# A separate drain for the last batch: pairs of token tiles, other PSUM banks, stores tile by tile

## The reference, cut to what matters

```
x = x + layernorm(attention(layernorm(x)))          # x: 8 batches x 512 tokens x 256 features, float32
x = x + layernorm(ffn(layernorm(x)))

def attention(x):
    q, k, v = split(x @ W_qkv.T)                    # 16 heads of 16 features; k is normalized over its 16
    for t in range(512):                            # a scan over the tokens, F is 16 x 16 per head
        F = retention * F + coef * outer(v[t], k[t])
        y[t] = (W_LTM + F) @ q[t]
    return y @ W_o.T

def ffn(x):
    h = relu(x @ W_fc.T) ** 2                       # 1024 hidden features
    y = h @ W_proj.T
    mem = 0                                         # 5 steps of a spiking unit on each element
    for step in range(5):
        mem = 0.9 * mem + y - (mem > 1)
        spikes += (mem > 1)
    return spikes / 5
```

## Time and profile before

| | us |
|---|---|
| median of 3 runs | 639.84 (638.00 to 641.08) |
| the profiled execution | 640.17 |
| its span, first to last instruction | 638.4 |
| TensorE busy | 498.8 (78%) |
| VectorE busy | 534.7 (84%) |
| ScalarE busy | 326.7 (51%) |
| GpSimd busy | 384.3 (60%) |

### The profile page before, as it was taken

How to read it: one execution, slowest core, us unless ns; L and a number is a source line. 1 busy time by engine, 2 the same in 40 slices (tenths; PEclk the granted TensorE clock), 3 DMA queues, 4 the chain that set the end, 5 groups by cost and what they waited for, 6 DMA issues and landing times.

```text
span 638.4 us, 7784 instructions
## 1 busy us (share of the span) xinstructions
PE 498.8 (78%) x2272; PEld 326.5 (51%) x2272; DVE 534.7 (84%) x937; ACT 326.7 (51%) x637; POOL 384.3 (60%) x184
## 2 busy tenths in 40 slices
PE   3583478449996999699979997899969995895891
PEld 1341135126673657355745665566636663473670
DVE  4799989997998999899999999999899999821001
ACT  4522123245546754656376646655567355646634
POOL 0026965785567776677677767875687667811101
PEclk9875589679897999989998999798979998988796
DMA  7364476465644575456545664567338634200000
GB/s 236 114 182 134 131 212 183 119 164 146 182 128 122 165 208 139 131 140 189 167 135 156 180 180 119 154 173 209 99 85 230 203 110 132 66 2 0 32 2 33
DMA packets 54729, 87.63 MB, mean 137 GB/s; under 512 B 5408, under 2 KB 19360, under 8 KB 54688
## 3 DMA queue, kind: packets, MB, share of 16 engines
q1 hardware_dynamic: 54112, 87.12, 48.2%
q10 hardware_dynamic: 576, 0.03, 0.1%
HBM read 78.74 MB, written 8.39 MB: 136 GB/s over the span
## 4 chain that ended last, share of the span: by engine, by line
PE 53%; issue 16%; POOL 10%; ACT 10%; DVE 10%; DMA 1%; POOLq 0%; ACTq 0%; DVEq 0%
PE p_c L346 13%; PE p_c L371 12%; PE p_a L281 7%; POOL prod L875 6%; PE p_y L324 6%; DVE state L733 5%; PE p_c L337 4%; ACT sign L547 3%; PE p_c L354 2%; PE p_a L301 2%; POOL x1t L891 2%; PE p_y L319 2%; DVE p_u L723 2%; ACT oo L468 1%; PE p_c L363 1%
## 5 line engine op out<-in xcount | busy, mean ns | idle before, releaser
L875 POOL TENSOR_TENSOR prod<-state,qf 128x1024 f32<-128x1024 f32 x128 | 302.8, 2371 | 147.5 <-DVE state L733 126.1
L733 DVE TENSOR_TENSOR_SCAN state<-ret,p_u 128x512 f32<-128x512 f32 x256 | 308.8, 1207 | 0.0
L723 DVE TENSOR_TENSOR p_u<-vrep,p_k 128x512 f32<-128x512 f32 x256 | 171.1, 674 | 2.5 <-ACT p_k L479 2.5
L346 PE MATMUL p_c<-wproj_sb,ht 128*128 128x256 f32 x512 | 116.1, 382 | 1.3 <-ACT ht L537 1.3
L371 PE MATMUL p_c<-x1t,wfc_s 128*128 128x512 f32 x384 | 99.4, 411 | 11.7 <-POOL x1t L891 10.6
L346 PEld LDWEIGHTS p_c<-wproj_sb,ht 128*128 128x128 f32 x512 | 95.7, 190 | 24.3 <-issue 9.2
L281 PE MATMUL p_a<-xt,wqkv_s 128*128 128x512 f32 x276 | 82.4, 437 | 13.9 <-POOL xt L891 5.4
L371 PEld LDWEIGHTS p_c<-x1t,wfc_s 128*128 128x128 f32 x384 | 74.4, 197 | 32.9 <-POOL x1t L891 13.7
L324 PE MATMUL p_y<-prod,summer 128*32 128x512 f32 x512 | 75.1, 661 | 8.5 <-POOL prod L875 8.5
L281 PEld LDWEIGHTS p_a<-xt,wqkv_s 128*128 128x128 f32 x276 | 53.1, 202 | 47.8 <-issue 16.3
L535 ACT ACTIVATE hr<-p_c 128x512 f32<-128x512 f32 x64 | 38.2, 597 | 36.8 <-PE p_c L371 34.9
(11 more groups left out here) (106 smaller groups left out, 481.0 us busy)
## 6 DMA issues: line engine op xcount, KB each, us to landing
vrep<-v_rows SPq DMA_DIRECT2D x256, 256.0 KB, 3.6
xa<-in_x SPq DMA_DIRECT2D x8, 512.0 KB, 5.4
v_rows<-vf SPq DMA_DIRECT2D x16, 256.0 KB, 2.0
x<-in_x SPq DMA_DIRECT2D x8, 512.0 KB, 4.7
out<-x SPq DMA_DIRECT2D x8, 512.0 KB, 3.4
ht<-in_w_fc SPq DMA_DIRECT2D x1, 1024.0 KB, 7.4
wproj_sb<-in_w_proj SPq DMA_DIRECT2D x1, 1024.0 KB, 9.9
state<-in_w_qkv SPq DMA_DIRECT2D x1, 512.0 KB, 5.5
```

What stands on the lines that cost most here:

```text
L346: last = pe.matmul(p_c[(u + 1) % 2][:, 0:D], ht[:, f, tokens(u)], wproj_sb[:, f, :], start=(f == 0), stop=(f == FT - 1))
L723: v.tensor_tensor(p_u[n % NU][:, :], vrep[:, n % NV, :], p_k[:, :], ALU.mult).then_inc(S["hebb_done"], 1)
L733: v.tensor_tensor_scan(state[:, s % NS, i, :], ret[:, r:r + 1].broadcast_to([P, L]), p_u[n % NU][:, :], 0.0, ALU.mult, ALU.add).then_inc(S ...
L875: p.tensor_tensor(prod[:, s % NZ, :, :], state[:, s % NS, :, :], qf[:, s // HS, :].unsqueeze(1).broadcast_to([P, 2, L]), ALU.mult).then_in ...
```

## The change

The last full iteration and what follows it are written anew for batches 6 and 7; the iterations before stay.

- In the last iteration, in which no next batch is prepared, batch 6's `up`s stand in slots 10 to 13, two in each, and `down` 0, 1 and 2 in slots 13, 14 and 15. ScalarE's `hidden` and `copy_yf` follow suit.
- The two iterations after it are gone. In their place every engine has a list of its own. It ends batch 6 (`down` 3, `count_spikes`, norm 4) with the old functions, between pieces of batch 7.
- Batch 7 goes through in pairs of tiles (256 tokens) up to `tail_up`, and tile by tile after. VectorE takes the moments of the out-projection from PSUM (`tail_attention_moments`), scales and adds it to x in one operation (`tail_attention`), scales for norm 3 (`tail_norm3`) and subtracts the high part (`tail_low`), both done by other engines before. `tail_up` has 12 matmuls of 256 columns for two times 128 hidden features; ScalarE has only the Relu, and VectorE multiplies it by the sum in PSUM, which is the square (`tail_hidden`). Four banks take turns.
- `tail_down` writes four different banks. Two of the five sign tensors of a tile are made by ScalarE and three by VectorE. The spikes' norm and add are on VectorE, from PSUM (`tail_spikes`), and each tile of 128 tokens has its own store of 128 KB.

The diff, cut to its core:

```diff
@@ run @@
             iteration(B - 1, True, True, True, False)
-            iteration(B, False, True, True, False)
-            iteration(B + 1, False, False, True, False)
...
+        LAST = B - 1
+        ON_ACT = 2
...
+        turn_bank = [p_a, p_y]
+        up_bank = [p_u[2], p_k, p_u[0], p_u[1]]
+        down_bank = [p_a, p_y, p_u[2], p_k]
+        count_bank = [p_c[0], p_c[1], p_u[0], p_u[1]]
@@ SyncE @@
-            store_out(B - 1)
...
+            for u in range(TILES):
+                sp.wait_ge(S["tail_res"], u + 1)
+                row = LAST * L + u * P
+                sp.dma_start(out[row:row + P, :], x1[LAST % 2][:, u, :]).then_inc(S["out_done"], 16)
@@ TensorE @@
+                    if not after:
+                        if 10 <= s < 14:
+                            up(b1, 2 * (s - 10))
+                            up(b1, 2 * (s - 10) + 1)
+                        if s == 13: down(b1, 0, False)
+                        if s == 14: down(b1, 1, False)
+                        if s == 15: down(b1, 2, False)
...
+            def tail_up(pair, fp):
+                n = 4 * pair + fp
+                pe.wait_ge(S["tail_low"], pair + 1)
+                pe.wait_ge(S["tail_h"], at(n - 3))
+                if n in (2, 3): pe.wait_ge(S["tail_x1"], n - 1)
+                for m in range(2):
+                    f = 2 * fp + m
+                    for t in range(KT):
+                        for i, j in PASSES:
+                            last = pe.matmul(part(up_bank[n % 4], m), wfc_s[:, i, t, f * P:(f + 1) * P],
+                                             x1t[:, j, t, pair_cols(pair)], start=(t == i == j == 0),
+                                             stop=(t == KT - 1 and i == 1))
+                last.then_inc(S["tail_up"], 1)
...
+            sums(LAST, 6)
+            down(LAST - 1, 3, False)
+            count_spikes(LAST - 1, 0)
+            sums(LAST, 7)
+            tail_out(0)
+            tail_out(1)
+            count_spikes(LAST - 1, 1)
+            tail_turn(0)
+            tail_up(0, 0)
+            tail_up(0, 1)
+            tail_turn(1)
+            tail_up(0, 2)
+            tail_up(0, 3)
+            for fp in range(4):
+                tail_up(1, fp)
+            tail_down(0)
+            tail_down(1)
+            tail_count(0)
+            tail_down(2)
+            tail_count(1)
+            tail_down(3)
+            tail_count(2)
+            tail_count(3)
@@ VectorE @@
+            def tail_attention(pair):
+                dve.wait_ge(S["n2_done"], TILES * LAST)
+                tail_reciprocal(2, 2 * pair, 2, pair + 1)
+                dve.wait_ge(S["again_in"], 16 * B)
+                for i in range(2):
+                    u = 2 * pair + i
+                    last = v.scalar_tensor_tensor(x1[LAST % 2][:, u, :], part(p_u[pair], i), rdev[1][:, u:u + 1],
+                                                  x1[LAST % 2][:, u, :], ALU.mult, ALU.add)
...
+            def tail_hidden(pair, fp):
+                n = 4 * pair + fp
+                dve.wait_ge(S["tail_relu"], n + 1)
+                dve.wait_ge(S["down_done"], TILES * LAST)
+                v.tensor_tensor(ht[:, 2 * fp:2 * fp + 2, pair_cols(pair)],
+                                up_bank[n % 4][:, :].rearrange("p (f l) -> p f l", f=2),
+                                hr[:, n % 2, :].rearrange("p (f l) -> p f l", f=2), ALU.mult).then_inc(S["tail_h"], 1)
...
+            def tail_spikes(u):
+                dve.wait_ge(S["tail_count"], u + 1)
...
+                counted = count_bank[u][:, 0:D]
+                tail_moments(4, u, 1, [counted])
+                tail_reciprocal(4, u, 1, u + 1)
+                tail_step(v.tensor_scalar(spk[:, u, :], counted, moments[3][:, u, 0:1], rdev[3][:, u:u + 1], ALU.subtract,
+                                          ALU.mult))
+                v.tensor_tensor(x1[LAST % 2][:, u, :], x1[LAST % 2][:, u, :], spk[:, u, :], ALU.add).then_inc(
+                    S["tail_res"], 1)
...
+            tail_signs(0)
+            tail_signs(1)
+            tail_spikes(0)
+            tail_signs(2)
+            tail_spikes(1)
+            tail_signs(3)
+            tail_spikes(2)
+            tail_spikes(3)
```

More of the change, by code:

```diff
@@ L434, in iteration @@
                         turn_x1(b1, 1)
-                    if before:
+                    if before and after:
                         if s == 10: up(b1, 0)
@@ L443, in iteration, with tail_out @@
                             up(b1, 7)
-            run(iteration)
+                    if not after:
[5 more added lines that the diff above has]
+                        if s == 15: down(b1, 2, False)
+            run(iteration)
+            def tail_out(pair):
+                pe.wait_ge(S["y_done"], 2 * B)
+                for i in range(2):
+                    for half in range(HALVES):
+                        last = pe.matmul(part(p_u[pair], i), yt[:, half, tokens(2 * pair + i)], wo_sb[:, half, :],
+                                         start=(half == 0), stop=(half == HALVES - 1))
+                last.then_inc(S["tail_out"], 1)
@@ new lines, in tail_turn @@
+            def tail_turn(pair):
+                pe.wait_ge(S["tail_n3"], pair + 1)
+                for t in range(KT):
+                    for i in range(2):
+                        last = pe.transpose(turn_bank[pair][:, tokens(2 * t + i)],
+                                            oo[:, 2 * pair + i, t * P:(t + 1) * P], ident_sb[:, :])
+                last.then_inc(S["tail_turned"], 1)
+            def tail_up(pair, fp):
[5 more added lines that the diff above has]
+                    f = 2 * fp + m
+                    for t in range(KT):
+                        for i, j in PASSES:
[3 more added lines that the diff above has]
+                last.then_inc(S["tail_up"], 1)
@@ new lines, in _, with tail_deviation, tail_high @@
+            run(iteration)
+            def tail_deviation(n, first, count, number):
+                act.wait_ge(S[f"tail_var{n}"], number)
+                tiles = slice(first, first + count)
+                eps = eps_sb[:, 1:2] if n == 4 else eps_sb[:, 0:1]
+                nc.scalar.activation(dev[n - 1][:, tiles], moments[n - 1][:, tiles, 1], ACT.Sqrt, bias=eps).then_inc(
+                    S[f"tail_dev{n}"], 1)
+            def tail_high(pair):
+                act.wait_ge(S["tail_turned"], pair + 1)
+                nc.scalar.copy(x1t[:, 0, :, pair_cols(pair)],
+                               turn_bank[pair][:, :].rearrange("p (t l) -> p t l", t=KT)).then_inc(S["tail_high"], 1)
@@ new lines, in _ @@
+            copy_yf(LAST - 1, 2)
+            copy_yf(LAST - 1, 3)
+            copy_y(LAST, 1)
+            signs(LAST - 1, 1)
+            tail_deviation(2, 0, 2, 1)
+            tail_deviation(3, 0, 2, 1)
+            tail_deviation(2, 2, 2, 2)
+            tail_high(0)
+            tail_deviation(3, 2, 2, 2)
+            copy_count(LAST - 1, 0)
+            copy_count(LAST - 1, 1)
+            tail_relu(0)
+            tail_relu(1)
+            tail_high(1)
+            for n in range(2, 8):
+                tail_relu(n)
@@ L863, in _, with tail_step, tail_moments @@
             run(iteration)
+            tail_steps = [0]
+            def tail_step(ins):
+                tail_steps[0] += 1
+                ins.then_inc(S["tail_step"], 1)
+                dve.wait_ge(S["tail_step"], tail_steps[0])
+            def tail_moments(n, first, count, srcs):
+                for u, src in zip(range(first, first + count), srcs):
+                    last = v.bn_stats(stats[n - 1][:, u, :], src)
+                tail_step(last)
+                for u in range(first, first + count):
+                    last = v.bn_aggr(moments[n - 1][:, u, :], stats[n - 1][:, u, :])
+                last.then_inc(S[f"tail_var{n}"], 1)
@@ new lines, in _ @@
+            scan(LAST, SLOTS - 1, 1)
+            tail_attention_moments(0)
+            tail_attention(0)
+            tail_attention_moments(1)
+            tail_norm3(0)
+            tail_attention(1)
+            tail_low(0)
+            tail_norm3(1)
+            tail_hidden(0, 0)
+            tail_hidden(0, 1)
+            tail_low(1)
+            tail_hidden(0, 2)
+            tail_hidden(0, 3)
+            statistics(4, LAST - 1, spk, "spk_done", 2 * LAST)
+            for fp in range(4):
+                tail_hidden(1, fp)
@@ L919, in _ @@
             run(iteration)
+            read(LAST, SLOTS - 1)
+            add_feed_forward(LAST - 1)
 def constants():
```

107 lines of the change are left out of this document (100 added, 7 removed).

## The result

The changed kernel takes 625.14 us (median; 623.55 to 625.93) where the kernel before takes 640.46 beside it (638.00 to 642.86); both are medians of four runs. The ratio is 0.9757, with a 95% interval of 0.9730 to 0.9784. The profiled execution of after took 623.55 and has a span of 621.3, against 638.4.

A forecast was written before the change was run, and what follows sets the result against it. The bound was taken to be the scans until 555.46 us, then an 82.9 us drain with no engine but TensorE ever full. The new span of 624.4 is 14.0 less: 640.17 - 14.0 - 0.3 = 625.9, so 626; range 620 to 634.5.

The forecast's parts named there:

- Part 1: Batch 6's downs ahead of the last sums: `down` 0 near 556.0, copy of y 576.5, projection 16.6 us later.
- Part 2: From batch 7's out-projection to its first `up`: 10.0 us replace 31.1, of which 13.8 were the moved downs.
- Part 3: Batch 7's 96 `up` matmuls of 256 columns: 12.0 us, plus 0.4 for transposes and 2.5 for the clock.
- Part 4: Batch 7's downs and counts until 616.4, then signs, spikes and store until 624.4, 8.0 us after the last `down`.
- the late product of slot 14: In the drain, GpSimd's last two products end at 565.3, not 557.92, at no cost since TensorE is later still.
- The second clock charge: In batch 7's ups, six us at lowered clock do 28 matmuls and not 48: 2.5 us more.
- Rival B: In batch 7's ups, weight loads do not hide under 256 columns: 632 to 634.5 us, chance 0.13.
- The rule that the prediction set against this part: For batch 7's ups: weight loads overlap running matmuls only where the row group differs; 632 to 634.5 us.
- norm4 and GpSimd add hide beside the downs: In the drain, batch 6's norm 4 and add, before inside the ups, hide beside batch 7's downs.
- Rival C: In the drain, no clock loss and a short store: 620 to 622.5 us, chance 0.09.
- Rival E: In batch 7's ups, the exchange of banks leaves TensorE idle between groups: 634.5 to 641 us, chance 0.08.
- Rival D: The clock stays at half through the whole new drain: 647 us, slower than before, chance 0.04.

The follow-up runs named there:

- e1: The changed kernel with batch 6's four downs put back behind the last sums and batch 7's out-projection: 620.05 us, ratio 0.9672.
- e9: The kernel before with only batch 6's ups and downs, and ScalarE's work on them, moved into the last iteration: 645.66 us, ratio 1.0077.
- e6: The changed kernel with nine unread 256-column matmuls added in TensorE's idle time between projection and ups: 624.99 us, ratio 0.9737.
- e10: The changed kernel with batch 6's downs between and behind the last sums, GpSimd's add held until VectorE's tile 0 signs are made: 613.93 us.

## Why the prediction was right, point by point

The forecast of 626 against 625.14 is closer than its steps were. It expected the span 14.0 us shorter, at 624.4; it ended at 621.3. The 3.1 us lie as follows (-1.5 in part 1, 0 in part 2, -1.7 in part 3, +0.6 and -0.5 in part 4), and the profiled run was the fastest of the four, 1.6 below their median, with 2.3 us outside its span for before's 1.8. That these brought the forecast near again is luck.

- **Part 1.** Predicted: `down` 0 at 556.0, copy of y at 576.5. Measured 554.25 and 574.96. The lengths were right, 20.5 us predicted between the two and 20.7 measured, with 1.65 for the half clock (`down` 0 takes 5.11 us to sum 5's start, where sixteen records at 0.216 take 3.46) where 1.7 was charged; the ups had begun earlier, at 536.47 and not 538.10. That the late product of slot 14 costs nothing holds: sum 7 stood behind `down` 3 all the same.
- What the prediction did not ask is whether part 1 should be there at all. It booked 16.6 us of delay, and 13.8 us of `down`s gone from the relay, and went on. e1 and e9 priced it: a loss of 2.4 to 3.9 us behind the last scan and 3.7 to 6.1 in all in the traces, 4.6 to 5.1 in the medians. The missing thought is that a `down` behind the projection covers a relay, and one ahead of it covers only what TensorE would have idled there, 2.74 us.
- **Part 2.** Predicted 10.0 us, measured 9.97. Inside, errors cancelled: two fused multiply-adds took 0.88 and not 0.74, two scalings 0.62 and not 0.74. The steps with bank sources (480 and 544 ns) were over what was taken (370 and 420); the first stayed under its upper bound.
- **Part 3.** Predicted 14.9 us from the first `up` to the first `down`, measured 13.2. The spacing was 0.1175 for 0.125, at its lower bound. The second clock charge was the mis-sized term: the step took the two slow stretches of before, 6.7 us, as its model, and only one of 3.4 us came. Measured cost 1.3 us, not 2.5 (e6: 11.9 us with none). Rival B is out: each of these full-array matmuls has its own load (102 loads beside 101 matmuls in the window of the `up`s) and still costs what its columns do. The rule that the prediction set against this part stands on the page of the Trainium skill, "TensorE: Matmul & The Clock Gate", in the section "The mechanism", and not where the prediction put it. The trace contradicts its "only"; the same section also lets a load for the background weight buffer go ahead of running matmuls, and which of the two ways is taken here no run shows.
- **Part 4.** Predicted 15.0 for the `down`s and counts, measured 15.6; 0.5 of it is count 0 behind the slow signs (15.1 in e10). The step that failed is "norm4 and GpSimd add hide beside the downs": they hid from TensorE, and the add stood in VectorE's way. Predicted 8.0 from there to the end, measured 7.5 to 7.6: the store took 2.1 for 2.3, the rest was within 0.3.
- **The rivals.** Rival C did not come: the clock took 1.65 and 1.3 us, and the store 2.1. Rival E fell: between the first new `up` and the last `down` no idle time of TensorE exceeds 0.34 us. Rival D fell as well, though e9 shows that its mechanism lives near by: beside an idle time of 8.83 us the clock was down for 13.7.

Taken together from the table: the change delays the projection by 15.4 us, shortens the relay by 21.1, the `up`s by 3.6 and the end by 9, and lengthens the `down`s by 1.5. That is 16.9 us behind the last scan.

## What to carry to other kernels

When two pieces of work end a program, don't ask which can go first; ask which engine waits where, and lay the piece that needs no one into that wait. The four `down`s cost 3.7 to 6.1 us in the traces ahead of the last sums; with one in the wait before the last sum and three under VectorE's relay the kernel is 9 us faster than the changed one. A move and a rewrite that come in one change are to be priced apart: here the rewrite hid that the move lost.
